# Head sums of a chunk as 32x32 tiles over both PSUM banks with one chunk at a time, and projections issued in quarters

## The reference

```python
w = exp(-exp(w)).reshape(B, L, H, S)          # r, k, v likewise; H = 32, S = 16
def step(s, inp):
    k_l, v_l, w_l, r_l = inp
    a = k_l[..., :, None] * v_l[..., None, :]
    out = einsum('bhs,bhst->bht', r_l, faaaa * a + s)
    return a + w_l[..., None] * s, out
...
x = x + y * g @ Wo.T                          # y: outs, normalised by head
...
x = x + rr * (kk @ fWv.T)                     # rr = sigmoid(xr2 @ fWr.T), kk = relu(xk2 @ fWk.T) ** 2
```

## Time and profile before

| | |
|---|---|
| median of 3 runs | 921.98 us (920.86 to 922.21) |
| profiled execution: time | 921.95 us |
| profiled execution: span | 919.9 us |
| mean granted TensorE clock | 0.988 |
| PE busy | 870.7 us (95%), 6490 instructions |
| DVE busy | 639.5 us (70%) |
| ACT, POOL busy | 352.8 us (38%), 294.9 us (32%) |

### The profile page before, as it was taken

The page is one execution under the profiler, slowest core; times in us unless marked ns, Lnnn a source line. Parts: engine busy times, 40 slices in busy tenths (PEclk is TensorE's granted clock), DMA queues, the critical chain, the costliest instruction groups (busy, mean ns, idle before and its releaser), DMA issues.

```text
span 919.9 us, 16352 instructions
## 1 busy us (share of the span) xinstructions
PE 870.7 (95%) x6490; PEld 585.2 (64%) x6490; DVE 639.5 (70%) x1110; ACT 352.8 (38%) x715; POOL 294.9 (32%) x281
## 2 busy tenths in 40 slices
PE   7699999799999999999998999999999999999997
PEld 5477568457764686557764676646865577457674
DVE  3357966898479836997379954898468965986341
ACT  1222145523553146423363243531464236316422
POOL 3033641374107520373105720175202730640000
PEclk9799999899999999999999999999999999999999
DMA  8820102000010001100021000200001000000010
GB/s 309 307 69 0 47 20 75 1 1 1 2 69 24 1 2 60 56 1 1 2 70 47 1 1 2 93 23 1 2 24 46 1 1 2 24 24 2 1 46 23
DMA packets 17020, 34.09 MB, mean 37 GB/s; under 512 B 2224, under 2 KB 3888, under 8 KB 16944
## 3 DMA queue, kind: packets, MB, share of 16 engines
q1 hardware_dynamic: 14048, 31.20, 9.5%
q10 hardware_dynamic: 2896, 1.84, 0.6%
HBM read 24.65 MB, written 8.39 MB: 36 GB/s over the span
## 4 chain that ended last, share of the span: by engine, by line
PE 65%; DVE 17%; issue 5%; POOL 5%; ACT 4%; DMA 2%; SPq 1%; DVEq 0%; POOLq 0%; ACTq 0%
PE PB L496 21%; PE PC L502 8%; PE CH L578 6%; PE PC L496 6%; POOL prod L1953 3%; PE CH L637 3%; PE CH L614 3%; PE PC L671 3%; PE PA L489 3%; DVE av L1550 2%; PE PB L371 2%; DVE RA L1520 2%; DMA sq_Wo<-in_square 2%; DVE xmix L1458 2%; DVE wprod L1505 2%
## 5 line engine op out<-in xcount | busy, mean ns | idle before, releaser
L1943 POOL TENSOR_TENSOR xmix<-xmix,xa 128x512 f32<-128x512 f32 x80 | 96.5, 1227 | 190.9 <-DVE xmix L1458 190.9
L578 PE MATMUL CH<-prod,ones 128*128 128x512 f32 x272 | 143.3, 627 | 14.6 <-DVE prod L1482 5.2
L1953 POOL TENSOR_TENSOR prod<-RA,K 128x512 f32<-128x512 f32 x112 | 132.3, 1196 | 68.2 <-DVE RA L1520 41.0
L1458 DVE SCALAR_TENSOR_TENSOR xmix<-PA,chan,sx 128x256 f32<-128x256 f32 x160 | 66.1, 475 | 47.9 <-PE PA L489 47.9
L578 PEld LDWEIGHTS CH<-prod,ones 128*128 128x128 f32 x272 | 47.2, 194 | 64.9 <-issue 35.9
L1550 DVE TENSOR_TENSOR av<-CH,vT 128x512 f32<-128x512 f32 x112 | 76.2, 681 | 14.2 <-PE CH L578 14.0
L1132 ACT ACTIVATE st<-av,half 32x512 f32<-32x512 f32 x64 | 74.6, 1166 | 20.9 <-DVE av L1595 19.5
L1556 DVE TENSOR_REDUCE yred<-av 128x64 f32<-128x512 f32 (+2 forms) x112 | 76.9, 686 | 3.9
L496 PE MATMUL PC<-sqb,sq_fWk 128*128 128x256 f32 x256 | 58.6, 383 | 2.4 <-DVE sqb L1674 2.4
L496 PE MATMUL PB<-xmix,sq_Wg 128*128 128x256 f32 x256 | 58.5, 382 | 0.0
L496 PE MATMUL PB<-xmix,sq_Wr 128*128 128x256 f32 x256 | 58.5, 383 | 0.0
(11 more groups left out here) (162 smaller groups left out, 1407.2 us busy)
## 6 DMA issues: line engine op xcount, KB each, us to landing
x<-x_rows SPq DMA_DIRECT2D x11, 512.0 KB, 3.3
x<-in_x SPq DMA_DIRECT2D x8, 512.0 KB, 3.9
x_rows<-x SPq DMA_DIRECT2D x8, 512.0 KB, 3.4
out_x<-x SPq DMA_DIRECT2D x8, 512.0 KB, 2.7
ctx_t<-in_ctx SPq DMA_DIRECT2D x5, 512.0 KB, 4.9
y<-in_ctx SPq DMA_DIRECT2D x3, 512.0 KB, 8.1
sq_Wk<-in_square SPq DMA_DIRECT2D x1, 1024.0 KB, 13.1
sq_Wv<-in_square SPq DMA_DIRECT2D x1, 1024.0 KB, 16.4
```

Of the source, the lines that this page charges most:

```text
L578: pe.matmul(CH[:, (g % 2) * CHUNK:(g % 2 + 1) * CHUNK], ones16[:], prod[:, g % 3, :], start=True, stop=True).then_inc(chunk_mm, 1)
L1458: i = dve.scalar_tensor_tensor(xmix[:, SLOT_OF[name], ct, :], PA[:, ct * L:(ct + 1) * L], vec("maa_" + name, ct), sx[:, ct, :], ALU.add, A ...
L1943: pool.tensor_tensor(m, m, xa[:, ct:ct + 2, 1:L + 1], ALU.add).then_inc(mix_ready, 1)
L1953: pool.tensor_tensor(by_pair(prod[:, g % 3, :], h), r, k, ALU.mult).then_inc(prod_pool, 1)
```

## The change

- **Tiles.** A chunk is no longer one product of 128x128 by 512 columns but eight products of 32x32 by 256 columns: for each group of 32 rows q one on the diagonal (first half of the chunk, into the second half of CH's first bank) and one a column group further, (q + 1) mod 4 (second half of the chunk, into the first half of CH's second bank). The weights are the 32x32 diagonal blocks of `ones16`.
- **One chunk at a time.** A chunk takes columns 256 to 767 of CH, and chunk g waits for the weighing of chunk g-1.
- **Rotation.** In the second half of a chunk the channels come out 32 partitions further. So the columns of Wv for channels 256 to 511 are rolled by 32 on the host, `vT` and `yint` hold these channels rotated, and `turn_values` turns them back with a wider identity (`ident`, 160 columns).
- **Strided chunks.** Chunk c of a level takes every h-th block instead of a contiguous stretch, so that each chunk has as many columns in channels 0 to 255 as in 256 to 511.
- **Quarters.** The projections and `a_phi_g` are issued in twice as many parts, with the same instructions and semaphores.
- **Order.** All engines' orders are written anew, SP's too. The iterations of TensorE, VectorE and SP are shown below; the others change in the same way.

```diff
 def pairs(t, h, c, odd):
-            nb = CHUNK // (h * h)
-            v = t.rearrange("p (n two h) -> p n two h", two=2, h=h)
-            return v[:, c * nb:(c + 1) * nb, odd, :]
+            return t.rearrange("p (n c two h) -> p n c two h", c=h, two=2, h=h)[:, :, c, odd, :]
...
+            def turn_values(values, t):
+                for ct in range(CT):
+                    lo = 32 * (ct // 2)
+                    mm = pe.matmul(CH[:, t * C + ct * P:t * C + (ct + 1) * P], values[:, ct * L + t * P:ct * L + (t + 1) * P],
+                                   ident[:, lo:lo + P], start=(ct == 0), stop=False, is_transpose=True, skip_group_check=True)
+                return mm
...
-            def columns_half(out, half, w, rhs, signal):
-                for mt in [2 * half, 2 * half + 1]:
-                    for kt in range(CT):
-                        mm = pe.matmul(...)
-                mm.then_inc(signal, 1)
+            def columns_tile(out, mt, w, rhs, signal):
+                for kt in range(CT):
+                    mm = pe.matmul(out[:, mt * L:(mt + 1) * L], w[:, kt, mt * P:(mt + 1) * P], rhs[:, kt, :],
+                                   start=(kt == 0), stop=(kt == CT - 1))
+                if mt % 2:
+                    mm.then_inc(signal, 1)
...
 def b_chunks(u, lo, hi):                      # TensorE
-                    if g >= 2:
-                        pe.wait_ge(av_ready, N_CHUNKS * u + g - 1)
+                    if g:
+                        pe.wait_ge(av_ready, N_CHUNKS * u + g)
                     elif u:
                         pe.wait_ge(yn_ready, TT * u)
-                    pe.matmul(CH[:, (g % 2) * CHUNK:(g % 2 + 1) * CHUNK], ones16[:], prod[:, g % 3, :],
-                              start=True, stop=True).then_inc(chunk_mm, 1)
+                    for q in range(4):
+                        for turn in range(2):
+                            rows, o = slice(32 * q, 32 * (q + 1)), 32 * ((q + turn) % 4)
+                            h = slice(turn * CHUNK // 2, (turn + 1) * CHUNK // 2)
+                            mm = pe.matmul(CH[o:o + 32, (turn + 1) * CHUNK // 2:(turn + 2) * CHUNK // 2], ones16[rows, rows],
+                                           prod[rows, g % 3, h], start=True, stop=True)
+                    mm.then_inc(chunk_mm, 1)
...
 def b_weigh(u, g):                            # VectorE
-                src = CH[:, (g % 2) * CHUNK:(g % 2 + 1) * CHUNK]
+                src = CH[:, CHUNK // 2:3 * CHUNK // 2]
...
-                    dve.tensor_reduce(yred[:, c * n:(c + 1) * n], by_pair(dst, h), AX.X, ALU.add).then_inc(red_ready, 1)
+                    o = yred[:].rearrange("p (n c i) -> p n c i", c=h, i=h)[:, :, c, :]
+                    dve.tensor_reduce(o, by_pair(dst, h), AX.X, ALU.add).then_inc(red_ready, 1)
...
 # TensorE, iteration(i), from the gate projection to b_turn_k: before
-                a_gate(b2, 0); a_turn(b1); a_gate(b2, 1); b_reads(b3, 1); c_value(b4, 0); c_value(b4, 1)
-                b_chunks(b2, 0, 2); c_turn_y(b3, 0); b_chunks(b2, 2, 3); a_ranks(b1); c_turn_y(b3, 1); b_chunks(b2, 3, 4)
-                a_mix(b1, 0); b_chunks(b2, 4, 5); c_wo(b3, 0); b_chunks(b2, 5, 6); a_decay(b1); b_chunks(b2, 6, 8)
-                a_mix(b1, 1); a_decay2(b1); c_wo(b3, 1); b_chunks(b2, 8, 9); a_mix(b1, 2); b_chunks(b2, 9, 10)
-                a_key(b1, 0); c_turn(b3, 0); b_chunks(b2, 10, 12); c_turn(b3, 1); a_key(b1, 1); b_chunks(b2, 12, 13)
-                a_mix(b1, 3); b_chunks(b2, 13, 14); c_key(b3, 0); b_chunks(b2, 14, 17); c_key(b3, 1); b_turn_k(b2)
 # and after
+                a_gate(b2, 0); c_value(b4, 0, 1); a_turn(b1); b_reads(b3, 1); a_gate(b2, 1); a_gate(b2, 2); a_gate(b2, 3)
+                c_value(b4, 1, 0); b_chunks(b2, 0, 1); c_value(b4, 1, 1); c_turn_y(b3, 0); a_ranks(b1); b_chunks(b2, 1, 3)
+                c_turn_y(b3, 1); b_chunks(b2, 3, 4); a_mix(b1, 0); b_chunks(b2, 4, 5); c_wo(b3, 0, 0); b_chunks(b2, 5, 6)
+                a_decay(b1); b_chunks(b2, 6, 7); a_mix(b1, 1); b_chunks(b2, 7, 8); c_wo(b3, 0, 1); a_decay2(b1)
+                b_chunks(b2, 8, 9); c_wo(b3, 1, 0); b_chunks(b2, 9, 10); c_wo(b3, 1, 1); b_chunks(b2, 10, 11)
+                a_mix(b1, 2); a_key(b1, 0); c_turn(b3, 0); b_chunks(b2, 11, 12); c_turn(b3, 1); b_chunks(b2, 12, 13)
+                a_key(b1, 1); b_chunks(b2, 13, 14); a_key(b1, 2); a_key(b1, 3); c_key(b3, 0); b_chunks(b2, 14, 15)
+                c_key(b3, 1); b_chunks(b2, 15, 16); c_key(b3, 2); b_chunks(b2, 16, 17); c_key(b3, 3); b_turn_k(b2)
+                # then a_mix(b1, 3), a_value in quarters around b_turn_v and b_sums(b2, 0), a_mix(b1, 4), ...
...
 # VectorE, iteration(i)
-                b_prod(b2, 0); b_prod(b2, 1); c_out(b4, 1); b_chunks(b2, 0, 3); c_gate(b3, 0); ...
-                b_chunks(b2, 8, 10); c_z(b3, 0); c_z(b3, 1); a_mix(b1, 2); b_chunks(b2, 10, 12); c_shift(b3)
-                b_chunks(b2, 12, 17); a_mix(b1, 3); ...; a_shift(b0); a_gate(b1); b_norm(b2, 1); b_normed(b2, 0)
-                b_normed(b2, 1); c_out(b3, 0)
+                b_prod(b2, 0); b_prod(b2, 1); b_chunks(b2, 0, 1); c_out(b4, 1); b_chunks(b2, 1, 2); c_gate(b3, 0); ...
+                c_z(b3, 0); b_chunks(b2, 10, 11); c_z(b3, 1); b_chunks(b2, 11, 13); c_shift(b3); b_chunks(b2, 13, 14)
+                a_mix(b1, 2); b_chunks(b2, 14, 17); a_mix(b1, 3); ...; c_out(b3, 0); a_shift(b0); b_norm(b2, 1)
+                b_normed(b2, 0); b_normed(b2, 1); a_gate(b1)
...
 # SP, iteration(i)
-                keep_x1(f2); load_x(b1); load_ctx(f1); store(b5); bring_x1(b4)
+                store(b5); load_ctx(f1); keep_x1(f2); bring_x1(b4); load_x(b1)
```

More of the change, by code:

```diff
@@ L356, in drain @@
                 store(6)
+                keep_x1(7)
                 bring_x1(7)
@@ L376, in a_phi_g @@
                 out, c_in = layer1(s)[0], ctx_a if ahead(s) else ctx_t
-                if ahead(s):
+                if half:
+                    pass
+                elif ahead(s):
                     pe.wait_ge(ctx_ahead, 16 * (AHEAD.index(s) + 1))
@@ L389, in a_phi_g @@
                         pe.wait_ge(w_pg, 16)
-                for m in range(CT):
+                for m in [2 * half, 2 * half + 1]:
                     for kt in range(TT):
@@ L622, in b_reads @@
                     pe.wait_ge(U_ready, 8 * (u + 1))
-                for ct in range(CT):
-                    pe.matmul(CH[:, t * C + ct * P:t * C + (ct + 1) * P], yint[:, ct * L + t * P:ct * L + (t + 1) * P],
-                              ident[:], start=(ct == 0), stop=False, is_transpose=True, skip_group_check=True)
+                turn_values(yint, t)
                 if u == B - 1:
@@ L832, in iteration @@
-                c_key(b3, 1)
-                b_turn_k(b2)
+                b_chunks(b2, 13, 14)
+                a_key(b1, 2)
+                a_key(b1, 3)
+                c_key(b3, 0)
+                b_chunks(b2, 14, 15)
+                c_key(b3, 1)
+                b_chunks(b2, 15, 16)
+                c_key(b3, 2)
+                b_chunks(b2, 16, 17)
+                c_key(b3, 3)
+                b_turn_k(b2)
+                a_mix(b1, 3)
+                a_value(b1, 0)
                 b_turn_v(b2)
-                a_value(b1, 0)
@@ L907, in drain @@
+                c_wo(6, 1, 0)
                 b_chunks(7, 7, 8)
@@ L938, in drain @@
                 c_key(7, 1)
-                c_receptance(7, 0)
-                c_receptance(7, 1)
-                c_value(7, 0)
-                c_value(7, 1)
+                c_key(7, 2)
+                c_key(7, 3)
+                c_receptance(7, 0, 0)
+                c_receptance(7, 0, 1)
+                c_receptance(7, 1, 0)
+                c_receptance(7, 1, 1)
+                c_value(7, 0, 0)
+                c_value(7, 0, 1)
+                c_value(7, 1, 0)
+                c_value(7, 1, 1)
             fill()
@@ L1791, in fill @@
                 b_normed(0, 1)
+                a_gate(1)
             def iteration(i):
@@ L1833, in iteration @@
                 b_normed(b2, 1)
-                c_out(b3, 0)
+                a_gate(b1)
             def drain():
```

592 lines of the change are left out of this document (338 added, 254 removed).

## The result

The changed kernel takes 936.05 us (median of 4 runs, 933.96 to 939.21), the kernel before in the same comparison 921.42 us (920.24 to 922.21). The ratio is 1.0163, with a 95% interval of 1.0125 to 1.0200: slower by 14.6 us, at the upper end of the range and on the side of the forecast. The execution that was profiled took 939.21 us with a span of 937.2 us; before's had 921.95 and 919.9.

A forecast was written before the change was run, and what follows sets the result against it. TensorE and VectorE were both taken as full in the chunk part, TensorE alone in the rest. Steady batches +7, batches 0 and 1 -0.6, drain +2 gave +8.5 on 921.95: 930.5 us, range 904 to 938.

The forecast's parts named there:

- The new chunk: On TensorE, a tiled chunk takes 0.51 us instead of 0.86, plus 0.09 us of draining per tiling change.
- TensorE's net: Over the run, tiles save 48 us and tiling changes cost 29.4, leaving 18.6 us, 2.3 us a steady batch.
- A steady batch: Chunk 0 to the next batch's chunk 0: 109.0 us against 107.3, 1.7 us slower, times four, 7 us.
- my table: Steady batch by parts, after against before: 43.2 against 41.7, 9.7 against 9.8, 56.1 against 55.8 us.
- VectorE as the bound of the chunk part: In the chunk part, VectorE's own work is what makes the single buffer cost time.
- two orders side by side: Old and new orders compared from chunk 0 to xk2_ready: 41.7 us before, 43.2 after, 1.5 later.
- 47.9 of 50.8 us: VectorE's busy time in a steady batch's chunk part before the change, given as why its work costs.
- c_out behind chunk 0 costs 0.8 us: VectorE idles 0.8 us in the chunk part because c_out waits for c_value's last quarter, begun after chunk 0.
- The fill: Before the first chunk: no term of its own; batches 0 and 1 were given -0.6 us together.
- The drain: Batches 6 and 7 and the tail: chunk parts +3, a shorter tail, +2 us in sum.
- rival 5: TensorE's clock falls to 1.2 GHz in longer waits, 2.5 us per 5 us stretch: 936 to 950 us, chance 0.05.
- the 18.6 us forecast for TensorE's work: TensorE's saving over the run: 48 us from tiled sums less 29.4 us for tiling changes.

The follow-up runs named there:

- the run with the moves taken back: Changed kernel with the last quarter of c_value's second half and VectorE's c_out in front of chunk 0 again, as before: 939.0 us, ratio 1.0195.
- the last kernel: Changed kernel with chunk 3's multiply and first mix earlier on VectorE, before's fill order, chunk 0's products earlier, and TensorE's decay behind chunk 7: 929.71 us.

## Why the prediction was right, and where it was wrong

The side, and the range, were right: slower, 936.05 in 904 to 938. The forecast of 930.5 was 5.5 us short, and its own range of 925 to 936 ended where the result lies. By its steps:

- **The new chunk** (0.51 us + 0.09 of draining): 0.59 us measured. Right. The tiles do run side by side: one after another the eight would take 3.4 us (8 x 0.43). The Trainium skill says that a change of mode drains TensorE (TensorEngine Tiling (Array Packing), Key Properties), and the trace agrees with 0.09 us. By the Trainium skill's span model for packed tiles (TensorE: Matmul & The Clock Gate, Measured speedup vs the span model) the start would be 0.05 us less, which makes the chunk 0.55 us, an estimate; the trace sides with 0.59.
- **TensorE's net**, 2.3 us a batch (bounds 1.6 to 2.9): too small. TensorE's busy time in a steady batch at full clock falls by 3.3 to 4.0 us, from 104.1 to between 100.1 and 100.8. The count of changes is right (177 and 375 in the traces too). What was off most is the old chunk: 0.86 us was read where chunks stand next to each other or to transposes, while the 17 of batch 4 take 16.5 us from start to start, idle time left out, 0.97 each. Part of that are changes beside them, but the chunk at 381.27 takes 0.94 us to the start of the next work with no change on either side:

```profile
382.21 1.89 PE L470 MATMUL PB<-zbuf,maa_w 128*128 128x256 f32 x8
```

- **A steady batch**, 1.7 us longer: wrong in size. Measured at full clock 0, with falls 0 to 2.9. The added waits were forecast as some 4 us and are 3.3 to 4.0 (idle 3.3 us a batch before, 6.6 to 7.3 after); it is the saving against them, 3.3 to 4.0 instead of 2.3, that was mis-sized. By parts: chunk 0 to c_key 42.6 us in batches 2 and 4 (forecast 43.2), c_key to b_turn_k 9.4 (9.7), b_turn_k to the next chunk 0 55.4 (56.1). Each part is a little shorter than in my table. The waits at chunks 2, 3, 4 and 5 were forecast as 1.8, 0.8, 1.2 and 1.6 us and are 0.95, 0.45, 1.65 and, at full clock, 1.81, so the places were right and the sum (5.4 against 4.9) nearly, though chunk 2 has half of what was said. The wait at chunk 0 is 0.48 us, not 0.75.
- **VectorE as the bound of the chunk part**: the mechanism was named too broadly. Taking 7 us of work from it gives a steady batch 0.4 to 0.6 us. Shown is that TensorE waits for single steps at the head of the part, through the order of VectorE's queue: in the run that moved the multiply of chunk 3 forward, chunk 4 starts at 10.66 us instead of 12.36. My "two orders side by side" had followed that order and so came out near; the sentence about 47.9 of 50.8 us was a poor reason.
- **c_out behind chunk 0 costs 0.8 us**: wrong in sign, by the run with the moves taken back (108.3 against 107.4 us).
- **The fill** had no term at all, and no reason was given; batches 0 and 1 had -0.6 us. Measured: +8.3 together, of it 5.0 before the first chunk. I had looked at the steady part and passed over VectorE's order in the fill. Shown by the run with before's fill (5.4 us back before chunk 0).
- **The drain**, +2: +5.5 (3.2 and 2.3). Batch 7 and the end can be taken apart, for several runs have no fall there: 128.4 us before, 126.9 in the new order with two buffers, 131.4 with one, 129.2 with the tiles. So the order gains 1.4, the one buffer costs 4.5, the tiles return 2.2, and the clock of the profiled execution adds 1.5. For batch 6 no such set exists.
- **The clock**, rival 5 at 0.05, with "mine reach 1.8 us" as its reason: it should have had a large share, not as another outcome but as part of the forecast. Its condition came true, for the longest wait of a steady batch is 1.81 us; its chance was too low. Batches 0 and 5 and the end, the same work in runs without the falls, take 2.7, 2.9 and 1.5 us less, batch 3 0.4: 7.5 of the 17.3 us of the profiled execution. The rival's price, 2.5 us for some 5 us of it, is 0.5 us for each us at half clock; measured are 2.9 us for 6.8, 0.43.

The 8.5 us of the forecast and the 14.6 of the result are thus made up differently: the steady batches cost about half of what I said (3.5 for 7 us, nearly all of it the clock), fill and drain much more. That the total fell into the range owes something to luck, errors of opposite sign: steady batches priced too high, fill, drain and clock too low or not at all. (The sum as written gives 8.4, not 8.5, which changes nothing.)

The sum at the end: order and single buffer cost 25 us (of it steady batches 8.6, up to the first chunk 4.4, batches 0 and 1 4.2, batch 6 and the end 7.8), and the tiles give back 10, with falls of the clock that the plain sums did not have. That is less than the 18.6 us forecast for TensorE's work, and at full clock about half of the 3.7 to 4.4 us a batch that they take from it. Not tried were one buffer or tiles alone in the old order, and a tiled chunk with two buffers. In the latter both chunks would lie in the same two banks, a half each; what that would cost no run shows.

## What to carry to other kernels

A saving on the busiest engine that takes a buffer away is paid for in waits, and these waits follow the order of the other engine's queue, step by step: lay the two orders side by side instead of comparing busy times, and do so for the fill and the drain too, where most of this loss was. Price the old operation by what it takes on average where it stands, not by its best case. Ask of each new wait not only how long it is but what stands behind it: if TensorE's clock falls there, the work behind it pays, unless a further wait swallows it. Where a wait can't be removed, a few products that nobody reads are worth trying, with the clock of each batch looked at rather than the total alone, and in more than one execution.

## What the runs showed of the hardware

In every batch of the changed kernel TensorE waits several times in the first 17 us behind chunk 0, for 0.45 to 1.8 us each, and in or behind these waits the granted clock falls to half, the 1.2 GHz level, for 3.4, 6.8 or 10.2 us; in batch 5 it stays there until 25 us behind chunk 0, where nothing is waited for any more. The kernel before waits 0.75, 0.18, 0.55 and 0.72 us there (chunks 2 and 3, a_mix, a_decay) and keeps full clock in batches 2 to 5. Filling the waits of the last kernel with 2.6 us of matmuls a batch (six of 0.43) removed the falls from five of the six batches.

Waits alone do not settle it. The one-buffer run with 128x128 sums waits 0.88, 0.44, 0.87 and 1.58 us at the same chunks and shows no fall in any batch. The changed kernel, which differs from it only by the tiles, shows one in every batch, and the run with 128x128 sums and two buffers, with 4.7 us of idle time in most chunk parts, has one in each of the batches 1 to 6. Which of idle time, its placing and the lighter tiled work tips it is open. It also differs between equal batches of one execution: with fillers in the changed kernel, batches 2, 4 and 5 are free of it and batch 3 is not, and batches 0 and 7 of that run are free of it without fillers.
